# A fused attention and table-coded FFN kernel: two adds in the last group go from GpSimd to VectorE, and six loads are issued ahead of the counters' first increments

## The reference

```python
xn = _layernorm(x, axis=-1)
# attention: for each of 3 decays
scores = einsum('btd,bsd->bts', xn @ Wq, xn @ Wk[i]) * (decay ** expn * causal)
blended += gate[..., i:i + 1] * einsum('bts,bsd->btd', scores, xn @ Wv[i])
s = blended @ Wo * out_scale
# FFN: weights are lut[idx], 512 -> 1376 -> 512
g = silu((silu(xn @ lut[gate_idx].T) * (xn @ lut[up_idx].T)) @ lut[down_idx].T)
x = x + s * g
```

## Time and profile before

| | us |
|---|---|
| median of 3 runs | 1812.95 |
| lowest and highest | 1812.1, 1813.01 |
| the profiled execution, its own time | 1813.45 |
| its span, first to last instruction | 1811.5 |
| TensorE busy | 1773.3 |
| VectorE busy | 1379.0 |
| GpSimd busy | 1038.4 |
| ScalarE busy | 827.1 |

### The profile page before, as it was taken

How to read it: one execution, slowest core, us unless ns; L and a number is a source line. 1 busy time by engine, 2 the same in 40 slices (tenths; PEclk the granted TensorE clock), 3 DMA queues, 4 the chain that set the end, 5 groups by cost and what they waited for, 6 DMA issues and landing times.

```text
span 1811.5 us, 43135 instructions
## 1 busy us (share of the span) xinstructions
PE 1773.3 (98%) x16520; PEld 1476.6 (82%) x16520; DVE 1379.0 (76%) x2719; ACT 827.1 (46%) x1442; POOL 1038.4 (57%) x1041
## 2 busy tenths in 40 slices
PE   5999999999999999999999999999999999999997
PEld 2337888888888988888888888888898888888886
DVE  7897877777786878777787777778687777868684
ACT  3785444444444444454444444444444444444433
POOL 9303746656474755647474664647476564747263
PEclk9999999999999999999999999999999999999999
DMA  9986686968868686877968696886959687786753
GB/s 224 331 306 167 178 226 164 258 170 211 217 173 232 175 241 168 239 192 186 229 172 231 169 262 165 208 218 173 237 163 253 166 225 199 184 238 166 214 153 108
DMA packets 411033, 370.99 MB, mean 205 GB/s; under 512 B 222576, under 2 KB 278640, under 8 KB 410752
## 3 DMA queue, kind: packets, MB, share of 16 engines
q1 hardware_dynamic: 399824, 361.36, 73.2%
q0 software_dynamic: 11008, 6.89, 2.5%
HBM read 294.34 MB, written 35.52 MB: 182 GB/s over the span
## 4 chain that ended last, share of the span: by engine, by line
PE 93%; ACT 2%; DMA 2%; POOL 1%; DVE 1%; issue 1%; POOLq 0%; SPq 0%; DVEq 0%; ACTq 0%
PE F L1931 52%; PE F L1994 20%; PE B L1825 7%; PE F L1975 2%; PE B L1857 2%; PE B L1830 2%; PE B L1832 2%; PE B L1831 2%; PE F L1732 1%; POOL codes L756 1%; PE F L1830 1%; PE F L1831 1%; PE F L1832 1%; ACT ring L950 1%; DMA dblocks<-xt 1%
## 5 line engine op out<-in xcount | busy, mean ns | idle before, releaser
L1931 PE MATMUL F<-xtc,ring 128*128 128x256 f16 (+1 forms) x4224 | 497.7, 273 | 0.0
L1931 PEld LDWEIGHTS F<-xtc,ring 128*128 128x128 f16 (+1 forms) x4224 | 415.9, 100 | 42.5
L1994 PE MATMUL F<-ring,region 128*128 128x256 f16 x3360 | 382.5, 273 | 0.0
L1931 PE MATMUL F<-xt,ring 128*128 128x256 f16 (+1 forms) x3168 | 377.2, 273 | 0.0
L1994 PEld LDWEIGHTS F<-ring,region 128*128 128x128 f16 x3360 | 327.9, 98 | 47.9
L1931 PEld LDWEIGHTS F<-xt,ring 128*128 128x128 f16 (+1 forms) x3168 | 310.9, 100 | 33.2
L950 ACT ACTIVATE region<-region 128x512 f16<-128x512 f32 (+3 forms) x304 | 160.3, 527 | 283.2 <-DVE region L1606 115.8
L860 POOL TENSOR_TENSOR region<-hs,region 128x1024 f16<-128x1024 f32 x80 | 175.2, 2190 | 104.2 <-ACT region L950 104.2
L950 ACT ACTIVATE region<-F 128x512 f32<-128x512 f32 (+1 forms) x200 | 114.7, 575 | 101.1 <-PE F L1931 50.6
L868 POOL TENSOR_TENSOR faded<-state,fade_tile 128x384 f32<-128x384 f32 x56 | 46.3, 827 | 180.7 <-DVE region L1504 180.7
L878 POOL TENSOR_TENSOR x_out<-x_out,region 128x512 f32<-128x512 f32 x64 | 84.4, 1318 | 96.9 <-DVE region L1677 96.9
(11 more groups left out here) (265 smaller groups left out, 3438.6 us busy)
## 6 DMA issues: line engine op xcount, KB each, us to landing
ring<-blocks SPq DMA_DIRECT2D x546, 256.0 KB, 3.3
ring<-dblocks SPq DMA_DIRECT2D x224, 256.0 KB, 3.4
x_next<-in_x SPq DMA_DIRECT2D x64, 256.0 KB, 3.7
x_out<-in_x SPq DMA_DIRECT2D x64, 256.0 KB, 3.2
out_y<-x_out SPq DMA_DIRECT2D x64, 256.0 KB, 5.5
ring<-blocks SPq DMA_DIRECT2D x112, 128.0 KB, 2.5
ring<-dblocks SPq DMA_DIRECT2D x112, 128.0 KB, 3.1
blocks<-ring SPq DMA_DIRECT2D x35, 256.0 KB, 7.0
```

The source lines that it names most:

```text
L1931: ins = T_.matmul(out_, a, b, start=fresh, stop=False, skip_group_check=True)
L1994: ins = T_.matmul(bank[:, j * HV:(j + 1) * HV], a, b, start=fresh, stop=False, skip_group_check=True)
```

## The change

Two edits. At the end of the last group VectorE makes the two last adds of x (`finish(2)`, `finish(3)`), each right behind the product that it adds; in the other 15 groups nothing moves. At the start SyncE issues its three small loads, and GpSimd its first three direct loads, ahead of the increments of the semaphores.

```diff
         @block.sync
         def _(sp):
+            sp.dma_start(lutrow[:, :], lut.partition_broadcast(P)).then_inc(s_small, 16)
+            sp.dma_start(dlog[:, :], decay_logits.partition_broadcast(P)).then_inc(s_par, 16)
+            sp.dma_start(oscale[:, :], out_scale.partition_broadcast(P)).then_inc(s_par, 16)
             for t in range(GT):
                 sp.sem_inc(s_y[t], 16 * FREE)
...
-            sp.dma_start(lutrow[:, :], lut.partition_broadcast(P)).then_inc(s_small, 16)
-            sp.dma_start(dlog[:, :], decay_logits.partition_broadcast(P)).then_inc(s_par, 16)
-            sp.dma_start(oscale[:, :], out_scale.partition_broadcast(P)).then_inc(s_par, 16)
...
         @block.gpsimd
         def _(pool):
             G_ = nc.gpsimd
+
+            def load_direct(b):
...
+            for b in range(UNR):
+                load_direct(b)
             pool.sem_inc(s_hl1, 2 * FREE)
             pool.sem_inc(s_hl2, 2 * FREE)
             pool.sem_inc(s_tt, 2 * NTT * FREE)
             pool.sem_inc(s_yr, FREE)
             pool.sem_inc(s_hsl, FREE)
...
-            for b in range(UNR):
-                load_direct(b)
...
-                finish(2)
-                finish(3)
+                if not last:
+                    finish(2)
+                    finish(3)
...
+                def finish(n):
+
+                    block, v0 = ((C22, HV), (C21, 0))[n - 2]
+                    to = x_out[:, 0:2, v0:v0 + HV]
+                    dve.wait_ge(s_y1, gi * GT + n + 1 + GT)
+                    dve.wait_ge(s_yr, gi * GT + n + FREE)
+                    V_.tensor_tensor(to, to, block, ALU.add).then_inc(s_yr, 1)
...
-                product_out(2)
-                product_out(3)
+                for n in (2, 3):
+                    product_out(n)
+                    if last:
+                        finish(n)
```

More of the change, by code:

```diff
@@ L739, in _ @@
             G_ = nc.gpsimd
+            def load_direct(b):
+                rows = idx[UNITS[b][1]].rearrange("p q c -> p (q c)").unsqueeze(1).broadcast_to([QR, CG, CG * BANK])
+                pool.dma_start(codes[b].rearrange("p q c -> p (q c)"), rows).then_inc(s_first[b], 16)
+            for b in range(UNR):
+                load_direct(b)
             pool.sem_inc(s_hl1, 2 * FREE)
@@ L744, in _ @@
             pool.sem_inc(s_hsl, FREE)
-            def load_direct(b):
-                rows = idx[UNITS[b][1]].rearrange("p q c -> p (q c)").unsqueeze(1).broadcast_to([QR, CG, CG * BANK])
-                pool.dma_start(codes[b].rearrange("p q c -> p (q c)"), rows).then_inc(s_first[b], 16)
-            for b in range(UNR):
-                load_direct(b)
             def cast(u, c, col, w, done):
```

## The result

The changed kernel takes 1807.23 us (median of 8 runs) against 1812.59 for the kernel before in the same comparison: ratio 0.9971, 95% interval [0.996, 0.9981], so 3.4 to 7.2 us less. Its profiled execution took 1807.25 us, with a span of 1805.4 where it was 1811.5. Single executions of one kernel differ by 2.5 to 5.5 us here, and an interval of some ten runs reaches 1.6 us to either side, so a smaller gain can be looked for only in the traces.

What follows compares the result with a forecast made beforehand. TensorE's work, 93% of the chain, is untouched; GpSimd's closing DRAIN sets the end, the casts' queue the start. 4.4 us (0.57 included) + 0.33 = 4.7 us takes 1812.95 to 1808.25; range 1806.8 to 1812.5.

Steps and rivals of the forecast that it cites:

- The end: After the last matmul: GpSimd's closing DRAIN sets the end; with it hidden, SyncE is last, 4.4 us less.
- The 0.57 us for the add: Last add of x on VectorE takes 0.69 us instead of GpSimd's 1.26, moving stores and SyncE's DRAIN 0.57 us earlier.
- The bound of 2.23 us: Upper bound for VectorE's add of x, from the median of a like add on line 1661; 0.69 us was taken.
- The weak step: GpSimd's DRAIN ends at 1802.9 once its last add is earlier; worth 3.8 us, bounds 0 and 3.8.
- the 6.8 us: Time by which GpSimd's closing DRAIN outlasts its last add, 1804.45 to 1811.24; no row said what it is spent on.
- The rival in which the DRAIN stays late: GpSimd's closing DRAIN again ends 6.8 us behind the last add or later; only 0.57 + 0.33 us won, 1812.05; 25%.
- The rule: Skill's rule of constant 12 ns or so closing DRAINs: nothing to hide at the end, the edit worth 0.57 us alone.
- The start's step: In the set-up the casts' queue decides and moves by what its first load moves: gain 0.33 us.
- The 0.63 us: Gap between GpSimd's five increments and its first load; if the load's own, that load starts 0.33 us earlier.
- The second rival: At the start, casts begin 1.38 us earlier as small loads clear the way before the direct loads: 1807.2; 12%.
- the slower rival: Small loads in front hold the first direct load and casts by up to 1.7 us, DRAIN stays late: 1814.1; 4%.
- The sign that the prediction named: VectorE's first comparison behind `xt` in the set-up at 38.7 instead of 39.02; wrong if later than 39.

Runs made afterwards that it cites:

- e6: The changed kernel with GpSimd only waiting at the end for VectorE's last add, no operation: 1812.03 us, ratio 1.0002 against the kernel before.
- e1: The kernel before with only the last group's two adds moved to VectorE: 1806.97 us against 1812.04, ratio 0.9974.
- m1: A kernel that only copies x to the output with SyncE's DMAs, no DMA on GpSimd, one closing GpSimd memset: GpSimd's closing DRAIN 181 ns.
- e3: The kernel before with only SyncE's three small loads moved ahead of its increments: 1813.16 us, ratio 1.0006.
- e4: The kernel before with only GpSimd's first three direct loads moved ahead of its increments: 1810.87 us, ratio 0.9996.
- e8: The kernel before with the adds on VectorE and GpSimd's direct loads in front, SyncE's loads left behind the increments: 1805.24 us against 1811.45, ratio 0.9965.
- e2: The kernel before with all first loads ahead of the increments, adds left on GpSimd: 1811.74 us against 1812.04, ratio 1.0.
- e9: The changed kernel measured once more against the kernel before: 1807.18 us, ratio 0.9973.

## Why the prediction was right

**The end was read rightly, and to 0.05 us.** It said that GpSimd's DRAIN sets the end; that it would be over at about 1802.9 in that time scale, 4 us ahead of SyncE; and that SyncE would be last: 4.37 us. Measured 4.42. The 0.57 us for the add came out as 1.26 - 0.69 = 0.57, and the missing 0.05 is the hand-over, 0.08 us from VectorE to GpSimd and 0.03 on VectorE itself. The bound of 2.23 us was not reached; GpSimd had no operation during either add.

**The weak step held, its reason did not.** The prediction allowed the 6.8 us as a cost behind the last operation, or as 8.08 us from the DRAIN's start, and took both as hidden by the edit. Both forms gave the same number, but e6 shows that the first is wrong: an idle GpSimd pays the same. What mattered was when the DRAIN starts, which the last waiting instruction on GpSimd decides, even a bare wait. The rival in which the DRAIN stays late (1812.05) is refuted by e1.

**The rule.** The trace of the changed kernel disagrees again, with GpSimd's 8092 ns, with the constant of some 12 ns that the Trainium skill ("VectorE: DVE Perf Modes", section "The DRAIN you can't avoid") gives, on all five engines, for the DRAINs of the runtime's own start and end code. SyncE's 13 ns agree, and m1 shows 181 ns for GpSimd at its shortest. These DRAINs stand on a line of the kernel (210), so it is not shown that the page means them; the measurement decides.

**The start's step named the right queue, but had the wrong size, and its worth in time can't be confirmed.** Taken: 0.33 us, since the casts' queue moves by what its first load moves. The 0.63 us behind GpSimd's increments did belong to the load: it starts at 1.27, 0.39 us earlier. VectorE's lead was lost in waits at `chalf` and `xt`, as said, though it was 3.4 us and not 1.38, for `lutrow` also lands 3.6 us faster when it is ahead of the direct loads. But the queue was ahead by about 1 us (0.2 MB at 15 us), not by its own 0.39.

The second rival gave a reason: the small loads get out of the direct loads' way. Between 5 and 10 us it looks so, where the kernel before moved 135 GB/s and the changed kernel moves this:

```profile
5.00:10.00 5.00, 0.32 (x4) 0.17 (x8) 4.58 (x22) 0.20 (x1) 5.00 (x10) 1.00 1.02 198
```

The stretch ahead of it tells the other part: 8 GB/s from 0 to 5 us, where it was 39 before. The stream starts later and is then undisturbed. With the small loads alone in front (e3) the queue has gained nothing by 15 us, and with them left behind (e4, e8) it gains as much as in the changed kernel. So that reason is not borne out, and the slower rival's loss of up to 1.7 us at the queue did not come either.

The sign that the prediction named, the first comparison behind `xt` (35.71, where 38.7 was forecast), proves little: the 39.02 it was counted from is the latest of three profiles with that start, and the others have 36.81 and 36.39. In time e2 gives no gain, with 1.6 us either way over eleven runs. What becomes of the queue's 1 us between 15 us and the first group is not settled.

**The sum.** Forecast 1808.25, measured 1807.23, or 1807.18 in e9. That lies 0.4 us below the spread that the forecast was given (1807.6 to 1809.1; by its own terms, 1812.95 - 4.37 - 0.8, the lower end is 1807.8), and on the second rival's 1807.2. This is no sign for that rival. The kernel before came out at 1812.59 in that comparison and not 1812.95, which is a third of the difference; as a gain it is 5.4 us there and 4.3 in e9 where 4.7 was forecast, and the adds alone (e1) have 5.1. The rest is inside the scatter. That the number came so near is owed to the 4.42 us at the end; the start's term added nothing that can be seen.

## What to carry to other kernels

Look at the closing instructions of every engine, which no view of busy time counts: the end is where the last DRAIN is over, not where the last store lands. In a kernel whose GpSimd has issued many DMAs, either let its last instruction (a wait included) come early enough, or put a DRAIN on it in idle time behind its last DMA; the second needs no work moved. A lead at the start of a set-up is worth only what the slowest of its queues lets through, and a median of ten runs cannot see it below some 1.6 us here. A single profile can't either where its rows scatter by as much: compare a count that doesn't, such as the bytes that a queue has moved, over all profiles with the same start.

## What the runs showed of the hardware that was not expected

A DRAIN on GpSimd takes about 80 to 90 ns for every DMA that GpSimd has issued since its last DRAIN: 181 ns with none, 270 with one, 5096 with 60, 6765 with 82. It takes them when it starts, however long the DMAs have been done: in e6 the last of them was issued 1.7 ms earlier. And small loads land in a different time by their place alone: `lutrow` took 6.2 us when it was issued 0.45 us behind GpSimd's first load, and 2.6 us when 0.5 us ahead of it (2.6 in e3 too, which moves only these loads). The gain is not free: the direct loads' stream then starts later, and by 10 us GpSimd's queue has moved 0.80 MB in e3 where it had moved 0.86.
